# Splitting queries and keys of a paged attention: from GpSimd to ScalarE and VectorE

## What is computed

```
x = x + L0(x)                      # weights picked per sequence
x = x + L1(x)                      # base weight plus picked low-rank adapters
q, k, v = x Wq', x Wk', x Wv'      # 32 query heads, 8 key/value heads, 128 wide
q, k = rope(rmsnorm(q)), rope(rmsnorm(k))
k_all = [16 pages of 32 cached keys, the 32 own keys]      # 544 columns
v_all = likewise
o = softmax(mask(q k_all' / sqrt(128))) v_all              # 4 query heads share a key head
x = x + o Wo'
x = x + L3(x)                      # weights picked per sequence
```

## Time and profile before

| | before |
|---|---|
| median of the runs | 2406.7 us (2405.97 to 2408.63, 3 runs) |
| span of the profiled execution, its own time | 2408.5 us |
| TensorE busy | 2319.6 us, 96% |
| VectorE busy | 1763.3 us, 73% |
| ScalarE busy | 1629.7 us, 68% |
| GpSimd busy | 1411.4 us, 59% |
| DMA | 455.94 MB, mean 189 GB/s |

### The profile page before, as it was taken

One profiled execution on the slowest core, in us unless ns is written; L12 is line 12 of the kernel. 1 busy time (PEld: TensorE's weight loads), 2 busy tenths in 40 slices (PEclk: granted clock), 3 DMA queues, 4 the chain that ended last, 5 costly groups with the idle time before them and its releaser, 6 DMA issues.

```text
span 2408.5 us, 57141 instructions
## 1 busy us (share of the span) xinstructions
PE 2319.6 (96%) x14624; PEld 2006.1 (83%) x14624; DVE 1763.3 (73%) x5422; ACT 1629.7 (68%) x4605; POOL 1411.4 (59%) x2250
## 2 busy tenths in 40 slices
PE   8999999999998899999999999999999999998999
PEld 5778888888887788888888888888888888887777
DVE  3435777777778887887887887887887887886332
ACT  4324666666667887887887887887877877876221
POOL 1003444444447787887877877877877877872000
PEclk9999999999998999999999999999999999999999
DMA  4335333333348677876867867767767767775332
GB/s 162 95 110 165 98 101 102 117 98 101 101 120 265 207 239 221 257 231 220 262 226 226 260 226 229 255 223 236 251 223 234 251 219 241 248 220 191 109 131 100
DMA packets 347958, 455.94 MB, mean 189 GB/s; under 512 B 34506, under 2 KB 280842, under 8 KB 343695
## 3 DMA queue, kind: packets, MB, share of 16 engines
q1 hardware_dynamic: 308398, 315.83, 41.6%
q0 software_dynamic: 36864, 134.23, 17.0%
q10 hardware_dynamic: 2528, 4.29, 0.5%
HBM read 374.53 MB, written 79.69 MB: 189 GB/s over the span
## 4 chain that ended last, share of the span: by engine, by line
PE 65%; POOL 15%; issue 10%; ACT 6%; DVE 2%; DMA 1%; POOLq 0%; ACTq 0%; SPq 0%; DVEq 0%
PE S L1168 22%; PE bank L1236 8%; PE S L1251 7%; PE S L1209 7%; PE bank L1251 7%; PE bank L1092 7%; POOL k_lo L281 5%; POOL q_hi L546 4%; POOL regK L511 4%; POOL q_lo L548 3%; PE S L1122 2%; ACT regC L720 2%; PE bank L1245 2%; ACT regC L762 1%; ACT regC L756 1%
## 5 line engine op out<-in xcount | busy, mean ns | idle before, releaser
L1236 PE MATMUL bank<-regC,regK 128*128 128x128 f32 x4096 | 548.7, 277 | 31.9 <-DVE oT_lo L992 24.4
L1236 PEld LDWEIGHTS bank<-regC,regK 128*128 128x128 f32 x4096 | 507.4, 192 | 56.8 <-DVE oT_lo L992 36.0
L974 DVE CUSTOM_DVE_ANT_0 regC<-S,mask 128x544 f32<-128x544 f32 x512 | 367.8, 718 | 143.9 <-issue 139.1
L714 ACT CAST k_hi<-regK 128x544 fp32r<-128x544 f32 x512 | 330.4, 645 | 183.6 <-PE S L1209 165.2
L1092 PE MATMUL bank<-ident,regC 128*128 128x128 f32 x2688 | 409.3, 275 | 12.7 <-DVE regC L986 9.1
L720 ACT ACTIVATE regC<-regC,nmx 128x544 f32<-128x544 f32 x512 | 384.7, 751 | 44.7 <-DVE nmx L974 31.8
L1092 PEld LDWEIGHTS bank<-ident,regC 128*128 128x128 f32 x2688 | 320.8, 140 | 110.4 <-issue 66.9
L531 POOL TENSOR_TENSOR regC<-regC 128x256 f32<-128x256 f32 x320 | 244.4, 785 | 277.9 <-DVE regC L943 277.9
L546 POOL TENSOR_TENSOR q_hi<-regC,ones 128x128 fp32r<-128x128 f32 x512 | 262.5, 513 | 223.5 <-PE S L1209 219.8
L943 DVE SCALAR_TENSOR_TENSOR regC<-S,rstd,regK 128x128 f32<-128x128 f32 x1280 | 345.9, 343 | 16.7
L281 POOL TENSOR_TENSOR k_lo<-regK,k_hi 128x192 fp32r<-128x192 f32 x512 | 342.3, 669 | 12.6 <-ACT k_hi L714 12.6
(11 more groups left out here) (124 smaller groups left out, 3934.9 us busy)
## 6 DMA issues: line engine op xcount, KB each, us to landing
regK<-kT_cache SPq DMA_DIRECT2D x1024, 128.0 KB
qkT_d<-regC SPq DMA_DIRECT2D x160, 256.0 KB, 2.3
regC<-qkT_d SPq DMA_DIRECT2D x64, 512.0 KB
oT_d<-regC SPq DMA_DIRECT2D x64, 256.0 KB
regK<-oT_d SPq DMA_DIRECT2D x16, 1024.0 KB, 5.5
regC<-wqk SPq DMA_DIRECT2D x10, 1024.0 KB, 5.4
v_d<-regC SPq DMA_DIRECT2D x32, 256.0 KB, 2.3
regK<-qkT_d SPq DMA_DIRECT2D x64, 128.0 KB
```

What stands on the lines that cost most here:

```text
L974: nc.vector.tensor_tensor_reduce(out=p_sb[u % 4], in0=scores[u % 2], in1=mask[u // HK % 2][:], scale=-SCALE, scalar=3e38, op0=ALU.add, op1 ...
L1236: last = nc.tensor.matmul(oP[:, j * P:(j + 1) * P], v_sb[b][:, m, u % HK * D:(u % HK + 1) * D], pT_sb[u % 2][:, m * P:(m + 1) * P], start= ...
```

## The change

The split of the queries leaves GpSimd. ScalarE now rounds the queries of four heads at once, 128x512, by a cast (q_hi), and VectorE subtracts for the four heads at once (q_lo). Both do so at steps 0, 4, 8 and so on, ahead of their part of `split_k`, for heads u+4 to u+7. VectorE makes the keys' low half whole, 544 columns. GpSimd keeps the gathers and the copies of indices. q_hi and q_lo still have two buffers, of four heads each; the tiles are laid out anew in the same region. TensorE's `score` waits for queries once in four heads. SyncE loads queries and own keys apart: the queries behind `s_qp`, the own keys behind `s_klo` with the pages.

```diff
-            def split_q(n, u, pair):
-                b, h = u // HK % 2, u % HK
-                if h == 0:
-                    pool.wait_ge(s_k[b], pair * KLOAD + KLOAD)
-                ge(pool, s_qk, n - 1)
-                q = q_sb[b][:, h * P:(h + 1) * P]
-                nc.gpsimd.tensor_tensor(q_hi[u % 2], q, ones[:], ALU.mult).then_inc(s_qhi, 1)
-                pool.wait_ge(s_qhi, n + 1)
-                nc.gpsimd.tensor_tensor(q_lo[u % 2], q, q_hi[u % 2].bitcast(F32), ALU.subtract)
-                pool.wait_ge(s_khi, n + 1)
-                k_low(nc.gpsimd, b, h, u, slice(LOW, NPP + 1)).then_inc(s_qp, 1)
...
+            def split_q(m, u, pair):
+                b, h = u // HK % 2, u % HK
+                if h == 0:
+                    act.wait_ge(s_k[b], pair * KLOAD + KLOAD)
+                ge(act, s_qk, m * 4 - 4)
+                nc.scalar.copy(q_hi[u // 4 % 2], q_sb[b][:, h * P:h * P + HW]).then_inc(s_qhi, 1)
...
                 if not (fixed and n + 4 >= NU):
+                    if u % 4 == 0:
+                        split_q(g * (UG // 4) + (u // 4 + 1), u + 4, g * 2 + (u + 4) // (2 * HK))
                     split_k(n + 4, u + 4, g * 2 + (u + 4) // (2 * HK))
...
-                k_low(nc.vector, b, h, u, slice(0, LOW)).then_inc(s_klo, 1)
+                lo, hi = (k[u % 2].rearrange("p (s t) -> p s t", t=PSIZE) for k in (k_lo, k_hi))
+                nc.vector.tensor_tensor(lo, k_sb[b][:, :, h, :], hi.bitcast(F32), ALU.subtract).then_inc(s_klo, 1)
+
+            def split_q(m, u):
+                b, h, i = u // HK % 2, u % HK, u // 4 % 2
+                dve.wait_ge(s_qhi, m + 1)
+                nc.vector.tensor_tensor(q_lo[i], q_sb[b][:, h * P:h * P + HW], q_hi[i].bitcast(F32), ALU.subtract)\
+                    .then_inc(s_qp, 1)
...
-                        sp.wait_ge(s_qp, g * UG + HK * (k + 1))
-                        load_own(b, k % 2)
+                        sp.wait_ge(s_qp, g * (2 * BT) + 2 * (k + 1))
+                        load_q(b, k % 2)
                         sp.wait_ge(s_klo, g * UG + HK * (k + 1))
+                        load_own_k(b, k % 2)
                         load_pages(b, k % 2)
...
-            def score(n, u):
+            def score(n, u, m):
 
                 pe.wait_ge(s_klo, n + 1)
-                pe.wait_ge(s_qp, n + 1)
+                if u % 4 == 0:
+                    pe.wait_ge(s_qp, m + 1)
```

More of the change, by code:

```diff
@@ L40 @@
 KW = (NPP + 1) * PSIZE
+HW = 4 * P
 QKB = HQ // 4 + HK // 4
@@ L175, in build @@
         oT_hi = parts("oT_hi", H2 * P)
[L177 to L180, removed]
+        q_hi, q_lo = [parts("q_hi0", HW)], [parts("q_lo0", HW)]
+        k_hi = [parts("k_hi0", KW)]
         po_sb = [inC(P) for _ in range(2)]
+        assert at[0] <= 12 * T
+        at[0] = 12 * T
+        k_lo = [None, parts("k_lo1", KW)]
+        k_hi.append(parts("k_hi1", KW))
+        q_hi.append(parts("q_hi1", HW))
+        q_lo.append(parts("q_lo1", HW))
         p_next = [inC(KW) for _ in range(3)]
@@ L184, in build @@
         pTo_sb = inC(4 * P)
+        o_st = inC(T)
+        x2r = inC(T)
         oT_lo = parts("oT_lo", H2 * P)
-        at[0] = 27 * T
+        assert at[0] <= CSZ - 2 * KW
+        at[0] = CSZ - 2 * KW
         p_sb = [inC(KW)] + p_next
-        q_hi.append(parts("q_hi1", P))
-        q_lo.append(parts("q_lo1", P))
+        k_lo[0] = parts("k_lo0", KW)
         o3_hi, o3_lo = ((y, x) for x, y in zip((oT_hi, oT_lo), o3_parts))
         xy = [o_st, x2r]
-        ones = sb("ones", [P, P])
         mask = [sb(f"mask{i}", [P, KW]) for i in range(2)]
@@ L276, in tile @@
             return i + j // 4, j % 4, i * 4 + j
-        def k_low(engine, b, h, u, slots):
-            lo, hi = (k[u % 2].rearrange("p (s t) -> p s t", t=PSIZE)[:, slots, :] for k in (k_lo, k_hi))
-            return engine.tensor_tensor(lo, k_sb[b][:, slots, h, :], hi.bitcast(F32), ALU.subtract)
         @block.sync
@@ L286, in _ @@
             SP = [mybir.EngineType.SP]
-            for dst, src in ((cond[:], cond_row), (ids[:], id_row)):
+            for dst, src in ((cond[:], cond_row), (ids, id_row)):
                 sp.dma_start(dst, src).then_inc(s_ids, 16)
@@ L399, in _ @@
                     load_pages(1, 1, (t - 4) * 2, 2)
-            load_own(1, 1)
+            load_own_k(1, 1)
+            load_q(1, 1)
             load_own_v(1, 1)
@@ L538, in _ @@
                     add_halves(e, t)
-            def split_q(n, u, pair):
-                b, h = u // HK % 2, u % HK
-                if h == 0:
-                    pool.wait_ge(s_k[b], pair * KLOAD + KLOAD)
-                ge(pool, s_qk, n - 1)
-                q = q_sb[b][:, h * P:(h + 1) * P]
-                nc.gpsimd.tensor_tensor(q_hi[u % 2], q, ones[:], ALU.mult).then_inc(s_qhi, 1)
-                pool.wait_ge(s_qhi, n + 1)
-                nc.gpsimd.tensor_tensor(q_lo[u % 2], q, q_hi[u % 2].bitcast(F32), ALU.subtract)
-                pool.wait_ge(s_khi, n + 1)
-                k_low(nc.gpsimd, b, h, u, slice(LOW, NPP + 1)).then_inc(s_qp, 1)
             def step(g, u):
[L553 to L556, removed]
+                fixed = isinstance(g, int)
                 k, m = (u - 10) // HK, (u - 10) % HK
@@ L568, in _ @@
                 add_halves(QKB - 1, t)
-                if t in (NT - 4, NT - 2):
-                    u = (t - (NT - 4)) // 2
-                    split_q(u, u, 0)
-            for u in range(2, 4):
-                split_q(u, u, 0)
             pool.wait_ge(s_tq, QKB * NT)
@@ L771, in _ @@
                 if t in FIRST_AT:
+                    if FIRST_AT[t] == 0:
+                        split_q(0, 0, 0)
                     split_k(FIRST_AT[t], FIRST_AT[t], 0)
@@ L1198, in block_qk @@
                     if last and t == NT - LAG:
-                        score(0, 0)
-            def score(n, u):
+                        score(0, 0, 0)
+            def score(n, u, m):
                 pe.wait_ge(s_klo, n + 1)
-                pe.wait_ge(s_qp, n + 1)
+                if u % 4 == 0:
+                    pe.wait_ge(s_qp, m + 1)
                 ge(pe, s_mx, n - 1)
+                head = slice(u % 4 * P, (u % 4 + 1) * P)
                 halves = (slice(0, 9 * PSIZE), slice(9 * PSIZE, KW))
-                for m, (q, k) in enumerate(((q_hi, k_hi), (q_hi, k_lo), (q_lo, k_hi))):
+                for i, (q, k) in enumerate(((q_hi, k_hi), (q_hi, k_lo), (q_lo, k_hi))):
                     for at in halves:
-                        last = nc.tensor.matmul(scores[u % 2][:, at], q[u % 2], k[u % 2][:, at],
-                                                start=(m == 0), stop=(m == 2))
+                        last = nc.tensor.matmul(scores[u % 2][:, at], q[u // 4 % 2][:, head], k[u % 2][:, at],
+                                                start=(i == 0), stop=(i == 2))
                 last.then_inc(s_qk, 1)
@@ L1267, in step @@
                 if not (fixed and n + 2 >= NU):
-                    score(n + 2, u + 2)
+                    score(n + 2, u + 2, g * (UG // 4) + (u + 2) // 4)
                 if u % 4:
@@ L1289, in _ @@
             block_qk(QKB - 1, 1, True)
-            score(1, 1)
+            score(1, 1, 0)
             pe.wait_ge(s_qT, QKB * NT)
```

21 lines of the change are left out of this document (11 added, 10 removed).

## The result

The changed kernel takes 2500.1 us, median of 4 runs (2490.3 to 2501.6), against 2407.7 for the kernel before in the same sitting: ratio 1.0375, 95% interval 1.0356 to 1.0394. The prediction was 2405, in a range of 2382 to 2425, with the trade of waits the likeliest; the change came out 92 us slower, outside the range.

The account below looks back on a forecast made before the run. No engine's total decides; six waits of three kinds per 32-head group count. G -1.89, E +1.30 and L +0.54 sum to -0.05 us a group, -1 us over 15 groups: 2405 us, range 2382 to 2425.

Parts of the forecast that it names:

- the trade of waits: Attention loop: GpSimd's waits are exchanged for ScalarE's and VectorE's, -0.05 us a group, 2390 to 2422 us; chance 68%.
- G: Score waiting for GpSimd before steps 16 and 24: both waits vanish, minus 1.89 us a group.
- E: Values waiting for ScalarE's copy of turned probabilities, steps 9, 17, 25: 0.61 us each, plus 1.30 a group.
- The lead: ScalarE and VectorE, freed of GpSimd, reach steps 16 and 24 early, sparing waits at 17 and 25: 18 us less.
- the faster rival: ScalarE and VectorE come early to steps 16 and 24, no copy wait at 17 and 25: 2387 or 2379; 17%.
- L: Values waiting for VectorE's oT_lo, steps 13, 21, 29: from 0.66 to 0.84 us each, plus 0.54 a group.
- the third rival: Contention on VectorE isn't GpSimd's and stays, oT_lo waits at their upper end: 2434 us; 13% shared with the gathers' rival.
- The shorter waits: Smaller waits in a group, left as they are, with 0.5 us a group either way.
- The rest: Remaining parts, including query waits, loads and four gathers in a row from step 8, needed eight heads later: no cost.
- The slower rival: Four gathers in a row at steps 8, 16, 24 delay VectorE's scalings 0.18 each: 32 us, 2437; 13% shared with staying contention.

Follow-up runs that it names:

- paced kernel: Changed kernel with gathers one per head's step again, the second to fourth each waiting for a head's k_hi, index copied column by column: 2404.6 us, ratio to before 0.9988.
- half rows: Changed kernel with four gathers still back to back, each of 64 rows instead of 128, values multiplied over 64 places: 2715 us, a time the study calls unusable.

## Why the prediction was wrong, step by step

The paced kernel has the change without the row of gathers, so the sum's terms are read there. Waits are spacings over the 0.44 and 0.81 us of the earlier trace rows.

**G** was to vanish, 1.89 us. It did: no score waits for GpSimd in any kernel with the split moved away.

**E** was to be 0.61 at steps 9, 17 and 25. It is 0.63, 0.62 and 0.63: 1.87 us against 1.83. ScalarE of the paced kernel, step 8, and TensorE into step 9:

```profile
1501.06 0.60 ACT L703 CAST q_hi<-regC 128x512 fp32r<-128x512 f32 x1
1501.56 0.64 ACT L695 CAST k_hi<-regK 128x544 fp32r<-128x544 f32 x1
...
1503.13 0.60 PE L1096 MATMUL bank<-ident,regC 128*128 128x128 f32 x4
...
1504.19 1.13 PE L1242 MATMUL bank<-regC,regK 128*128 128x128 f32 x8 [0.47 <-issue]
```

k_hi begins 0.50 after the cast, where the row of the weights' cast had 0.51; the Trainium skill's 224 cycles ("VectorE: DVE Perf Modes", TRN2 errata) would have put it at 0.61. The lead does not survive: the faster rival falls.

**L** was to be 0.84 three times. It is 0.89. Before, it was 0.58, 0.66 and 0.66, not 0.66 three times as the sum took it, so L grew by 0.77 us a group and not by 0.54. The chain from the small scaling to oT_lo was to take 1.79 and takes 1.81:

```profile
1511.93 0.24 DVE L987 TENSOR_SCALAR regC<-regC,rinv 128x32 f32<-128x32 f32 x1
...
1512.08 0.48 DVE L988 TENSOR_SCALAR regC<-regC,rinv 128x512 f32<-128x512 f32 x1
1512.47 0.68 DVE L967 TENSOR_TENSOR q_lo<-regC,q_hi 128x512 fp32r<-128x512 f32 x1
...
1513.07 0.75 DVE L961 TENSOR_TENSOR k_lo<-regK,k_hi 128x544 fp32r<-128x544 f32 x1
...
1513.74 0.68 DVE L994 TENSOR_TENSOR oT_lo<-bank,oT_hi 128x512 fp32r<-128x512 f32 x1
```

So the contention was GpSimd's tensor work and left with it; the third rival falls. The shorter waits, left open by 0.5 us, gave about 0.5 back. Together 5.44 us of waits a group where 5.73 were: -0.3, predicted -0.05. For this trade the 2405 stands: 2404.6. That it comes so close is in part luck: L's excess and the shorter waits, each worth 3 to 8 us over the run, work against each other.

**The step that failed** is the sentence on the gathers in "The rest": they stand in a row, are needed eight heads later, and so cost nothing. That asks only who waits for the gathers. It doesn't ask what they keep others from while they are issued. On before's trace they stood some 3 us apart because GpSimd's splits lay between them; the splits were their pacing. In a row they hold TensorE's score signal of heads 12, 20 and 28; the turnings of steps 11, 19 and 27 come 2.0 us late each (median of twelve groups), and the waits for oT_lo two steps on grow from 0.89 to 1.02. The fourth row, beside the output projection, holds signals up to 1.9 us and costs nothing: from the score of head 32 to that of head 43 the scores are spaced as in the paced kernel, to 0.01 us. That is 6.6 us of a group's 97.3, against 90.7 in the paced kernel; times 14 to 15 groups, the 95 us. A part of it is TensorE's clock: right after nine of these late turnings, ahead of which it has stood still for some 1.9 us, its granted clock falls to 0.5 (1.2 GHz) for 3.4 us, as at 1186.0; the paced kernel's loop has no such fall between 785 and 2211 us. At 1.7 us each these are at most 15 of the 95 us (an estimate from the lengths).

**The slower rival** named the right instructions and the right place, four gathers in a row at steps 8, 16 and 24, and the wrong victim: scalings of VectorE, 0.18 each, 32 us. The timeline of the changed kernel shows that pair of scalings beside a gather 0.14 apart, not 0.32, and so do all its 53 pairs beside gathers between 900 and 2100 us (0.15): the gathers don't hold VectorE's scalings at all. Its mechanism was read from a row in which GpSimd's tensor work and a gather came together, and took the one for the other; the four pairs in the trace of before that have a gather and no tensor work beside them stand 0.15 apart. Its chance, 13% with a bound of 2437, was too small by the size of the victim: everybody waits for TensorE's score, two engines at once.

## What to carry to other kernels

Work that is taken off an engine may have been the spacing of what remains on it. List the instructions that the change leaves next to each other, and if the trace has never shown them back to back, their price is unknown, not nothing; pacing them (a wait, or small work between) was cheap here. When two engines idle at once on the same producer that is already working on something later, suspect the signal, check its landing in the semaphore records, and look at what runs on the other engines in that window.

## What the hardware showed that was not expected

- Indirect gathers, four in a row and 1.22 to 1.36 us apart (medians), held TensorE's semaphore signals up to 2.7 us, and up to 3.2 with 64 rows; with three 1.56 to 1.87 apart and the fourth 2.4 to 2.6 behind, 1.04 at most, and two in a row 0.49 at most. How long a signal is held depends also on when in the row it falls due. What lies behind stays open.
- Only TensorE's signals were held. Of 250 to 290 recorded of each of three kinds from ScalarE and three from VectorE, in the same 900 us of the changed kernel, none landed more than 0.02 us after its instruction's end, and ScalarE's casts, copies and exponentials and VectorE's maxima and subtractions last as long as in the paced kernel. The Trainium skill, "Perfetto Trace Analysis", Tensor Engine Instruction, says that a matmul's update is pushed once PSUM acknowledges the write, after the modelled end. The held signals come after the modelled end, but no run shows whether the acknowledgement or the signal behind it is late.
- SyncE's register instructions, 0.04 us elsewhere, took up to 0.72 beside the gathers: 59 over 0.3 us in 900 us of the changed kernel, 15 in the kernel before, all of them within 2.5 us of a gather's start. Single gathers disturb it too: 29 in the paced kernel, up to 0.56.
- Matmuls over 64 places between matmuls over 128 lengthened each step by 0.37 us, at the full granted clock (half rows).
